# A fused attention and mixture kernel: probabilities of the first half turned on TensorE instead of a second pass, seven slots a span, another order in each slot

## The reference

```
q   = rope(rms_norm(layernorm(x)) as 16 heads of 32);  k = rope(rms_norm(ctx) as 4 heads);  v = ctx
a   = softmax(causal(q k^T / sqrt(32))) v              # 4 query heads share a key head
x   = x + a @ w_out^T
xt  = layernorm(x)
r   = top 4 of softmax(xt @ w_router), renormalized, times expert_scale     # 128 experts
mix = per expert 8 weights amplitudes^2, normalized; w = r @ mix            # 8 weights per token
u_k = silu(xt @ gate_k) * (xt @ up_k), k = 0..7; shared units 8 and 9 likewise
out = x + (sum_k w_k u_k) @ w_down + [u_8, u_9] @ shared_w_down
```

## Time and profile before

| | |
|---|---|
| time, three runs | 876.39, 870.22, 876.61 us; median 876.39 |
| profiled execution | 878.02 us, span 876.2 us |
| busy: TensorE, VectorE, ScalarE, POOL | 92%, 75%, 66%, 57% of the span |
| mean granted clock of TensorE | 0.978 |
| first projection starts | 88.3 us |

### The profile page before, as it was taken

How to read it: one execution, slowest core, us unless ns; L and a number is a source line. 1 busy time by engine, 2 the same in 40 slices (tenths; PEclk the granted TensorE clock), 3 DMA queues, 4 the chain that set the end, 5 groups by cost and what they waited for, 6 DMA issues and landing times.

```text
span 876.2 us, 15366 instructions
## 1 busy us (share of the span) xinstructions
PE 803.1 (92%) x4248; PEld 614.5 (70%) x4248; DVE 655.1 (75%) x1635; ACT 576.3 (66%) x1416; POOL 502.6 (57%) x682
## 2 busy tenths in 40 slices
PE   1566789989999998989999999998999999999997
PEld 1433567767777777767777787767777777787885
DVE  4635677777988985776979887786987775788774
ACT  1457677777777774667776775767787774555452
POOL 4555644987269634796449752897454522663471
PEclk9996889999999999899999999999999999999999
DMA  8013214455444446354454544544454435454650
GB/s 300 22 38 92 73 39 135 150 182 173 145 157 163 131 152 195 143 164 132 149 175 131 179 131 147 190 142 150 145 176 136 156 114 169 160 176 145 216 187 29
DMA packets 57859, 126.79 MB, mean 145 GB/s; under 512 B 12080, under 2 KB 28848, under 8 KB 57776
## 3 DMA queue, kind: packets, MB, share of 16 engines
q1 hardware_dynamic: 55952, 121.87, 42.4%
q10 hardware_dynamic: 1824, 3.94, 1.2%
HBM read 107.16 MB, written 4.19 MB: 127 GB/s over the span
## 4 chain that ended last, share of the span: by engine, by line
PE 60%; POOL 14%; SPq 6%; issue 6%; DVE 6%; ACT 3%; DMA 3%; ACTq 1%; POOLq 0%; DVEq 0%
PE u L1420 36%; PE u L1441 7%; SPq L540 4%; PE pair L1320 3%; PE o_bank L1336 3%; PE s L1308 3%; POOL macc L743 3%; POOL w_l L735 2%; PE u L1404 2%; POOL r_b L697 2%; PE pair L1323 1%; PE s L1356 1%; PE s L1388 1%; DVE w_l L1079 1%; DMA w_raw<-in_w_units 1%
## 5 line engine op out<-in xcount | busy, mean ns | idle before, releaser
L1420 PE MATMUL u<-w_h,t_h 128*128 128x512 f32 x640 | 267.1, 417 | 11.5 <-POOL w_l L735 7.6
L1420 PE MATMUL u<-w_h,t_l 128*128 128x512 f32 x640 | 251.6, 393 | 0.0
L1420 PE MATMUL u<-w_l,t_h 128*128 128x512 f32 x640 | 251.4, 393 | 0.0
L1079 DVE TENSOR_TENSOR w_l<-w_raw,w_h 128x512 fp32r<-128x512 f32 x288 | 248.7, 890 | 0.9 <-ACT w_h L774 0.9
L774 ACT ACTIVATE w_h<-w_raw 128x512 fp32r<-128x512 f32 x384 | 219.4, 622 | 19.3 <-DMA w_raw<-in_w_units 16.8
L735 POOL TENSOR_TENSOR w_l<-w_raw,w_h 128x512 fp32r<-128x512 f32 x96 | 134.8, 1404 | 130.4 <-ACT w_h L774 130.2
L1024 DVE CUSTOM_DVE_ANT_0 scores<-s,mask_qk 128x128 f32<-128x128 f32 (+3 forms) x256 | 123.4, 486 | 87.9 <-PE s L1308 85.6
L809 ACT ACTIVATE scores<-scores,mx 128x128 f32<-128x128 f32 (+3 forms) x256 | 142.8, 558 | 52.5 <-DVE mx L1024 51.5
L1420 PEld LDWEIGHTS u<-w_h,t_h 128*128 128x128 f32 x640 | 121.7, 190 | 45.1 <-issue 13.9
L743 POOL TENSOR_TENSOR macc<-macc,gb 128x256 f32<-128x256 f32 x112 | 112.6, 1007 | 56.6 <-DVE gb L1180 55.9
L1420 PEld LDWEIGHTS u<-w_h,t_l 128*128 128x128 f32 x640 | 120.9, 189 | 27.5
(11 more groups left out here) (146 smaller groups left out, 1169.7 us busy)
## 6 DMA issues: line engine op xcount, KB each, us to landing
w_raw<-in_w_units SPq DMA_DIRECT2D x156, 512.0 KB, 4.3
w_raw<-in_shared_w_down SPq DMA_DIRECT2D x16, 512.0 KB, 4.7
q_st<-turned_h SPq DMA_DIRECT2D x232, 32.0 KB, 1.9
w_raw<-in_w_out_t SPq DMA_DIRECT2D x14, 512.0 KB, 4.1
out<-x SPq DMA_DIRECT2D x16, 256.0 KB, 2.2
q_st<-turned_l SPq DMA_DIRECT2D x116, 32.0 KB, 1.9
x<-in_x SPq DMA_DIRECT2D x3, 1024.0 KB, 5.8
w_raw<-in_w_units ACTq DMA_DIRECT2D x4, 512.0 KB, 11.8
```

What stands on the lines that cost most here:

```text
L1079: e.tensor_tensor(w_l[:, i % WR, k, :], w_raw[:, i % WR, k, :], f32(w_h[:, i % WR, k, :]), ALU.subtract).then_inc(s_wl, 1)
L1420: last = e.matmul(u_bank[n % 2][:], t[:, k, cols], ww[:, i % WR, k, :], start=(k == 0 and m == 0), stop=(k == KC - 1 and m == 2))
```

## The change

1. Spans 0 to 3 have no second pass. Their masked scores go to a buffer of their own, `early`, for two spans; ScalarE's exponential with row sums writes the probabilities in place; TensorE turns them (12 transposes a span) into the banks of the second pass, and ScalarE copies them to `pr`. Maxima are split, turned and sent as rows only from span 4 on.
2. Spans of the first half of batch 0 take seven slots instead of four. All that follows starts twelve slots later, and the program begins eight slots earlier.
3. The reciprocal of the row sums is taken in the last slot of the first pass (`inverse=-1`), before in the second slot after it; its spreading moves from +2 to +1.
4. The load of batch 3's x leaves the slot that stores batch 0's last tile and gets one six slots later. That of batch 2's x moves ahead on SP.
5. The last pair's late units go in the order unit 7, 9, 7, 9 instead of 7, 7, 9, 9, and each tile is turned as soon as its units are done.
6. The order of the steps within a slot is another on every engine. On POOL the scales and the weights' low part now go ahead of the rope.

```diff
-SPAN = ((4, 6), (4, 8), (4, 8), (4, 7))
-FIRST, LAST = -32, 236
+SPAN = ((7, 6), (4, 8), (4, 8), (4, 7))
+FIRST, LAST = -40, 248
-CORE = dict(split=-1, inverse=1, maxima=0, spread=2, second_pass=3, inverse_turn=5,
+CORE = dict(split=-1, inverse=-1, maxima=0, spread=1, second_pass=3, inverse_turn=5,
             values=6, high=1)
-LEAD = dict(split=-1, inverse=0, maxima=1, spread=0, second_pass=3, inverse_turn=3, values=5, high=0, rope=-11, turn=0, stack=-3)
+LEAD = dict(inverse=-1, spread=1, second_pass=5, inverse_turn=4, values=9, high=0, rope=-11, turn=-1, stack=-1)
-LOADS = (-1, 15)
-START = (20, 44, 68, 92, 116, 140, 164, 188, 210)
+LOADS, XLOAD = (-7, 9), 8
+START = (32, 56, 80, 104, 128, 152, 176, 200, 222)
+                    if p == len(START) - 1 and n:
+                        at = LATE[1][0] + n - 1 + i
...
+        def masked_scores(u, m):
+            h, j, t, i = span(u)[1], m // TH, m % TH, u * G * TH + m
+            if u < KV:
+                return early[:, u % 2, j, t * (t + 1) // 2 * P:(t + 1) * (t + 2) // 2 * P]
+            return scores[:, i % AR, 0:(h * TH + t + 1) * P]
...
-                    if g % TT == TT - 1 and g // TT + XR < B:
-                        load_x(g // TT + XR)
...
+                for b in range(XR, B):
+                    if s == START[2 * (b - XR + 1)] + DOWN + XLOAD:
+                        load_x(b)
...
+                if u < KV:
+                    e.activation(pr[:, n % PR, 0:width], pair[:, 0:width], ACT.Copy).then_inc(s_ex, 1)
+                else:
+                    e.activation(pr[:, n % PR, 0:width], pair[:, 0:width], ACT.Exp, scale=-1.0).then_inc(s_ex, 1)
...
+            def turn_probabilities(u, k):
+                e.wait_ge(s_sum, (u + 1) * G * TH)
+                e.wait_ge(*p_free[0])
+                w = Q - seen(u, k)
+                for j in range(G):
+                    for t in range(k, TH):
+                        at = j * w + t * P - seen(u, k)
+                        last = e.transpose(pair[:, at:at + P], masked_scores(u, j * TH + t)[:, k * P:(k + 1) * P], ident[:])
+                last.then_inc(s_pb, 1)
```

More of the change, by code:

```diff
@@ L131, in attention_and_mixture_kernel @@
         xn = sb("xn", [P, 2, C])
+        with ExitStack() as before:
+            early = before.enter_context(nc.sbuf_tensor("early", [P, 2, G, TH * (TH + 1) // 2 * P], F32))
         macc, hs8, hs9 = sb("macc", [P, TT, I]), sb("hs8", [P, TT, I]), sb("hs9", [P, 2, I])
@@ L259, in core, with of_later_span @@
             return (LEAD if u < KV else CORE)[name]
+        def of_later_span(s, name):
+            for u in range(KV, NU):
+                if s == span_slot(u) + CORE[name]:
+                    return u
+            return None
         def of_span(s, name):
@@ L314, in moments_in @@
         def moments_in(s):
[L315 removed]
+            return [b * TT + t for b in range(B) for t in range(TT) if s == batch_slot(b) + MOMENTS[t if b == 0 else TT + t]]
         def mixture(s, name):
@@ L745, in pool_engine @@
             for s in slots:
+                if (hb := of_half(s, "key_scale")) is not None:
+                    key_scale(hb)
+                if (u := of_span(s, "spread")) is not None:
+                    spread_inverse(u)
+                if (g := mixture(s, "scales")) is not None:
+                    norm_scale(g)
+                if (hb := of_half(s, "query_scale")) is not None:
+                    query_scale(hb)
+                if (u := attended_before(s)) is not None:
+                    out_low(u)
+                for i, k in splits(s, "low"):
+                    if k in POOL_LOW:
+                        weights_low(i, k)
                 for k, part in ((1, rope_last), (0, rope_first)):
@@ L1241, in vector_engine @@
                     resident_low()
+                if (g := turned_down(s)) is not None:
+                    for k in range(2):
+                        down_low(g, k)
+                if (p := routing(s, "mix")) is not None:
+                    token_weights(p)
+                if (p := routing(s, "keep")) is not None:
+                    keep_largest(p)
+                for g in moments_in(s):
+                    moments(g)
                 if (p := routing(s, "coefficients")) is not None:
                     coefficients(p)
+                if (u := of_later_span(s, "split")) is not None:
+                    maxima_split(u)
+                if (g := mixture(s, "route")) is not None:
+                    logits(g)
+                for n in range(U0 + 1):
+                    if s == ROPE3[n]:
+                        rope_stacked(n)
+                if (u := of_span(s, "inverse")) is not None:
+                    inverse(u)
                 for i, k in splits(s, "low"):
@@ L1246, in vector_engine @@
                         weights_low(i, k)
-                if (p := routing(s, "mix")) is not None:
-                    token_weights(p)
-                for g in moments_in(s):
-                    moments(g)
-                for n in range(U0 + 1):
-                    if s == ROPE3[n]:
-                        rope_stacked(n)
+                if s == ONES:
+                    ones()
         def tensor_engine(e):
```

188 lines of the change are left out of this document (83 added, 105 removed).

## The result

The changed kernel takes 869.37 us (median of 20 runs, 866.40 to 872.36) and the kernel before 873.63 on the same chip (20 runs, 870.03 to 879.35): a ratio of 0.9942, interval 0.9925 to 0.9959. The change gave 4.3 us; 24.9 were forecast. All 20 runs lie above the forecast of 851.5 us and above the range of 842 to 866. The profiled execution of before, from which the forecast counts, is 4.4 us above its kernel's median over 20 runs, that of after (869.35 us, span 866.6) is at it. So the two traces differ by more (9.6 us by their spans, 8.7 by their times) than the kernels do.

The account below looks back on a forecast made before the run. Up to the first projection SP's DMA queue was taken as the bound, after it only TensorE's few waits counted. Terms of 11.8 + 2 + 6.3 + 6 + 0.8 - 2 = 24.9 us off 876.4 gave 851.5 us, range 842 to 866.

Parts of the forecast that it names:

- A: First half: spans 0 to 3 lose their rows DMAs and SP starts stacking earlier, so the first projection comes 11.8 us earlier.
- B: From 88 to 119 us, behind the first projection: waits on POOL's weight part and ScalarE's normalized x shrink, 2 us gained.
- C: Load of batch 3's x, six slots later: the next weights come earlier, a TensorE wait and half-clock time go, 6.3 us gained.
- E: Tail: reordered units put a product into TensorE's 0.84 us wait for the last gated part, 0.8 us gained.
- D: Middle: POOL computes the weight part ahead of the rope, so TensorE's waits for it shrink, 6 us gained.
- F: Earlier reciprocal: VectorE must wait for ScalarE's last sum in the twelve spans of 4 slots, 2 us lost.
- with the usual 1.2 us: Before the first projection: span 4's first second-pass product starts 1.2 us after SP issues its maxima rows, at 75.5 us.
- Rival 2: First half: the vector chain or POOL binds, so the first-half gain shrinks to 4 us: 859 us, chance 0.13.
- Rival 4: All 28 later spans: VectorE waits at the reciprocal, costing 50 us instead of 2: 900 us, chance 0.08.
- Rival 1: From 88.3 to 119.4 us: the projections start and stay at half clock, 9.4 us more: 861 us, chance 0.12.
- the rule against the change: First half: transposes don't count as clock activity, so the projections start with a colder array, the sum 9.4 us worse.
- Rival 3: Middle: new orders only exchange waits and the moved load collides elsewhere, so it gives nothing: 862.6 us, chance 0.12.

Follow-up runs that it names:

- the run with dense products: Dense bf16 products added in TensorE's waits of the first half, against the changed kernel with the key turn back: 863.59 us, ratio 0.9873.

## Why the prediction was wrong

By the medians, each good to some 2 to 4 us, the 4.3 us are made of: 9.9 (A and B), 5.1 (C), -9.0 (the key turn), -2.0 (E) and 0.3 left for D, F and the moved scales. Forecast were 13.8, 6.3, 0, 0.8 and 4.

- **The step that failed is one that is missing: the moved slots of the key turn were not priced.** `key_turn` at -17 beside a `key_stack` at -16 is in the change, and in no term of the sum. The forecast followed SP's queue in the first half and at the x load, and nowhere else. The rule that it had applied at the x load, that a thing standing ahead of weights in SP's queue holds them up, was the one that decided, at two other places. It cost 9.0 us, 11.7 put into the kernel before alone, and 8.4 in the traces both ways. The forecast's own mark of failure came up for it: from the first projection to the end it takes 786.8 us, over the 785 named, against 787.6 before. Of the 20.6 us that the gain falls short, 9.0 are this; 3.9 are A and B, 1.2 C, 2.8 E, 3.7 D and F. With this number alone put back the kernel takes 860.37 us, inside the range.
- **A, -11.8, measured -8.75 in the traces.** SP's side came within 1.4 us at its start and 0.3 at its end. What failed is "with the usual 1.2 us": the last link was not SP's rows but POOL's `o_l`, and the way there was made longer by the change itself (batch 1's key scale, query scale and moments in new slots: 1.3 us from SP's first stack to the projection, by the run that puts them back). Rival 2 had named POOL, but for span 4's rope, and with A at 4 us. The wait for it, 4.40 us before 51.98, is there. It is hidden from SP, as said (span 4's stack starts at 57.12); what it costs TensorE's own queue no run shows.
- **B, -2, measured -4.0.** From the first projection to pair 0's units it takes 30.8 us before (29.1 to 32.3 in the six kernels with the old first half) and 26.9 after. ScalarE's part of it, 2.47 us, fell to 1.63, and the wait for the weights' low part, 1.65, is gone. The bound was 4.1. The six old ones differ by 3.2 us among themselves, so the size is rough.
- **C, -6.3: right.** 5.1 us by the medians, 6.4 by the stretch; with the new first half 6.1 and 6.5.
- **D, -6, and F, +2: D hangs on the other orders, F does not show.** POOL's order undone alone costs 10.8 us, made alone gives nothing; the forecast took it as a thing of POOL's own. The forecast's caution, that a later rope can hold up a turn, came true: waits of 1.29 and 1.31 us for `r_b` at 375 and 575. For F, VectorE waits 6.2 us in 12 places, 0.7 at most, but the kernel loses nothing measurable by it: the stretch is 1.8 us shorter with the reciprocal undone everywhere and 1.1 from batch 1 on, each time with one stretch at half clock less, worth 1.7 us, in the trace. Rival 4, which needed over 0.95 us in each of 28, is refuted. And up to pair 0's units the earlier reciprocal gains: undone, it makes the kernel 5.0 us slower by the medians, 4.0 in the traces.
- **E, -0.8: not gained.** The wait for the last gated part went, and waits of 0.48 and 1.41 us at the units, for nothing that the profile shows, came in its place: 1.3 us lost in the traces, 2.0 by medians that the noise doesn't separate.
- **Rival 1, and the rule against the change.** The mean clock behind the projection was 0.88, not 0.5, so the rival did not happen. The Trainium skill (TensorE: Matmul & The Clock Gate, Part 4: PE-mode transpose) says that transposes don't count as activity for the gate. The traces agree only weakly: with plain products in the place of transposes two of the four groups of value products ran at full speed, with transposes none (its base) or one, and this is one trace. But the value products of the old first half, which turns no probabilities, ran at half already (1.51 us each four times), so there was little clock to lose. The forecast had taken the recorded 0.92 of the earlier trace rows for its speed.
- **Rival 3** had the right place, "any load ahead of weights shows", and gave the middle 0; with the key turn it was below 0. Its 0.12 was too little. Interactions of orders that were laid out together should have had more room than six separate bounds give.
- **The base.** 876.4 was the median of three runs; 20 give 873.6. This hides a part of the miss: counted from 873.6 the forecast would have been 848.7 us. The miss in time is 17.9 us, the miss in gain 20.6. The low end of the forecast's own range, 842, also needs B at its bound of 4.1; with A, D and F as stated it is 844.

## What to carry to other kernels

When a table moves, price every entry of it against the queue of the engine that issues DMAs: a stack of 8 us of issuing must end before the next weights are due, and neither a shorter wait nor another slot helps if it then stands in front of them (with the stack moved later the wait was gone and 7.5 us were lost). Judge a reordering as a whole and in its place: the same POOL order was worth 0 and 10.8 us. And end a chain at the instruction that starts the next stage, with all that it waits for, not at the engine that was the bound before.

## What the runs showed of the hardware

- The recorded clock can read 1.00 where the engine runs at half. In the kernel before it reads 1.00 up to 66 us, while sixteen value products take 1.51 us at 47.08 and 61.79, against 0.86 in others. These lie ahead of the first fall that the record shows; there the length of a repeating instruction is the measure.
- A float32 tile of 128x128 that is turned as a plain product with the identity is two instructions in the profile, and one as a transpose. Eight tiles take 2.02 us as sixteen plain products (69.88 in the run with plain products) and 1.04 us as eight transposes (57.99 in the run with dense products), both at full speed.
- A wait of 1.3 to 1.9 us can cost more than itself, and its length doesn't tell whether it does. In the changed kernel the clock was half for 3.4 us behind a wait of 1.90 us (280.48), which costs 1.7 us more, and full behind one of the same length (481.24; 1.00 from 480 to 490 us). Behind a wait of 1.29 us it was half for 3.4 us in the kernel with the last pair's old order and full in the kernel with the key turn back, which has the same code there:

```profile
371.44 0.44 PE L1287 MATMUL s<-ident,r_b 128*128 128x128 f32 x2 [1.29 <-POOL r_b L720]
```
```profile
370.23 0.44 PE L1290 MATMUL s<-ident,r_b 128*128 128x128 f32 x2 [1.28 <-POOL r_b L723]
```

  So two traces whose stretches differ by 1 to 2 us say nothing before their half-clock stretches are counted.
